# Packs of the last expert stage: the up weights are split in the chunk that a tile needs, and each tile waits for its own chunk

## The reference, cut to what matters

```python
H = D * 2 * 4 // 3          # 682; D = 256
h1 = jnp.einsum('bsd,ehd->ebsh', x, W1)
h2 = jnp.einsum('bsd,ehd->ebsh', x, W2)
eo = jnp.einsum('ebsh,edh->ebsd', jax.nn.sigmoid(h1) * h1 * h2, W3)
out = out + jnp.einsum('ebsd,bse->bsd', eo, weights)
```

## Time and profile before

| | us |
|---|---|
| median of three runs | 2204.55 |
| lowest and highest | 2202.09, 2207.64 |
| profiled execution | 2205.24 |
| its span, first to last instruction | 2203.4 |
| from PE's first up matmul of pack 0 to that of pack 38 | 562.37 |
| one such pack, mean | 14.80 |

### The profile page before, as it was taken

How to read it: one execution, slowest core, us unless ns; L and a number is a source line. 1 busy time by engine, 2 the same in 40 slices (tenths; PEclk the granted TensorE clock), 3 DMA queues, 4 the chain that set the end, 5 groups by cost and what they waited for, 6 DMA issues and landing times. The chain is left out here.

```text
span 2203.4 us, 38903 instructions
## 1 busy us (share of the span) xinstructions
PE 1618.1 (73%) x13182; PEld 1262.8 (57%) x13182; DVE 1422.0 (65%) x2628; ACT 704.8 (32%) x1457; POOL 798.5 (36%) x956
## 2 busy tenths in 40 slices
PE   5956766499975768622948996599588888888881
PEld 3545644377752445411634563488588888888881
DVE  4844555666646655541247885566498888888886
ACT  2311011245531434410312664111244444444440
POOL 1421103620014300103314301188566666666660
PEclk8978788689987887855968997699799999999995
DMA  3464615443116332291225321221355445544525
GB/s 103 161 176 124 184 46 148 157 122 114 48 58 184 73 69 68 61 307 61 63 67 170 104 81 37 68 92 66 140 179 177 155 164 177 173 152 171 181 100 191
DMA packets 286765, 274.02 MB, mean 124 GB/s; under 512 B 59033, under 2 KB 263676, under 8 KB 280958
## 3 DMA queue, kind: packets, MB, share of 16 engines
q1 hardware_dynamic: 274647, 249.09, 36.5%
q0 software_dynamic: 8688, 21.16, 2.7%
q10 hardware_dynamic: 3264, 1.57, 0.4%
HBM read 194.74 MB, written 79.35 MB: 124 GB/s over the span
## 5 line engine op out<-in xcount | busy, mean ns | idle before, releaser
L89 PE MATMUL psum<-e_x_split,e_up_split 128*128 128x256 f32 x2340 | 342.5, 300 | 103.7 <-POOL e_up_split L1788 103.7
L89 PEld LDWEIGHTS psum<-e_x_split,e_up_split 128*128 128x128 f32 x2340 | 319.7, 206 | 110.8 <-issue 87.9
L787 DVE TENSOR_REDUCE a_maxima<-psum 128x2 f32<-128x512 f32 x384 | 257.4, 687 | 160.1 <-PE psum L578 91.9
L1788 POOL TENSOR_TENSOR e_up_split<-e_up_raw,e_up_split 128x512 fp32r<-128x512 f32 x195 | 261.0, 1339 | 214.7 <-ACT e_up_split L1710 213.7
L758 ACT ACTIVATE a_probs<-psum 128x512 f32<-128x512 f32 x384 | 224.8, 598 | 265.6 <-PE psum L600 171.2
L1680 PE MATMUL psum<-e_down_split,e_hidden_split 128*128 128x256 f32 x1170 | 183.5, 295 | 0.8 <-DVE e_down_split L1745 0.8
L1731 ACT ACTIVATE e_silu<-psum 128x256 f32<-128x256 f32 x195 | 75.1, 385 | 325.2 <-PE psum L89 325.2
L1680 PEld LDWEIGHTS psum<-e_down_split,e_hidden_split 128*128 128x128 f32 x1170 | 163.1, 201 | 1.0 <-DVE e_hidden_split L1767 1.0
L578 PE MATMUL psum<-s_k_stack,s_q_stack 96*128 96x256 bf16 x512 | 123.0, 295 | 42.2 <-DMA a_rel_stack<-scr_r 30.0
L1767 DVE TENSOR_TENSOR e_hidden_split<-e_hidden,e_hidden_split 128x256 fp32r<-128x256 f32 x195 | 138.8, 712 | 6.7
L1039 DVE TENSOR_TENSOR a_products<-psum,mask 128x512 f32<-128x512 f32 x128 | 82.9, 686 | 77.6 <-PE psum L972 77.4
(11 more groups left out here) (246 smaller groups left out, 3170.6 us busy)
## 6 DMA issues: line engine op xcount, KB each, us to landing
e_up_raw<-in_w_ffn SPq DMA_DIRECT2D x39, 1280.0 KB, 7.5
e_down_raw<-in_w_ffn SPq DMA_DIRECT2D x39, 640.0 KB, 4.1
scr_q<-p_parts SPq DMA_DIRECT2D x40, 384.0 KB, 2.7
scr_k<-p_parts SPq DMA_DIRECT2D x40, 384.0 KB, 2.8
a_q_stack<-scr_q SPq DMA_DIRECT2D x96, 128.0 KB, 2.9
s_q_stack<-scr_q SPq DMA_DIRECT2D x96, 128.0 KB, 2.7
s_k_stack<-scr_k SPq DMA_DIRECT2D x96, 128.0 KB, 2.7
a_k_stack<-scr_k SPq DMA_DIRECT2D x84, 128.0 KB, 3.0
```

The lines of the kernel that those rows point to most:

```text
L89: last = eng.matmul(out, lhs(a, k), rhs(b, k), start=i == 0, stop=i == len(terms) - 1)
L787: dve.tensor_reduce(MX[:, u // 8, :, u % 8], s_bank(u), AX.X, ALU.max).then_inc(S["s_used"], 1)
L1788: pool.tensor_tensor(SU[:, r, 1, q], RU[:, r, q], SU[:, r, 0, q], ALU.subtract).then_inc(S["up_lo"], 1)
```

## The change

Both `high_up` and `low_up` now treat, as chunk m, the four runs of 128 columns that tile m needs, by a view of the buffer. Each instruction still handles 512 columns of 128 partitions. The view is of both parts of SU (e_up_split) and of RU alike, so that what is read lies where it is written. PE's wait ahead of tile c changes from the low parts of the whole pack to the first c + 1 low parts. No instruction is added, removed or moved on any engine, and all other waits stand, among them those by which ACT waits for a buffer to come free and SP for the low parts of a whole pack.

```diff
+        def tile_of(weights, m):
+            return weights.rearrange("p (w m n) -> p w m n", w=2 * KD, m=n_h)[:, :, m, :]
...
-                    pe.wait_ge(S["up_lo"], (i + 1) * n_h)
+                    pe.wait_ge(S["up_lo"], c + 1)
...
                 def high_up(i, m):
-                    r, q = i % 2, slice(m * UP, (m + 1) * UP)
+                    r = i % 2
...
-                    act.activation(SU[:, r, 0, q], RU[:, r, q], ACT.Copy).then_inc(S["up_hi"], 1)
+                    act.activation(tile_of(SU[:, r, 0], m), tile_of(RU[:, r], m), ACT.Copy).then_inc(S["up_hi"], 1)
...
                 def low_up(i, m):
-                    r, q = i % 2, slice(m * UP, (m + 1) * UP)
+                    r = i % 2
                     pool.wait_ge(S["up_hi"], i * n_h + m + 1)
-                    pool.tensor_tensor(SU[:, r, 1, q], RU[:, r, q], SU[:, r, 0, q], ALU.subtract).then_inc(S["up_lo"], 1)
+                    pool.tensor_tensor(tile_of(SU[:, r, 1], m), tile_of(RU[:, r], m), tile_of(SU[:, r, 0], m), ALU.subtract).then_inc(S["up_lo"], 1)
```

## The result

| | before | after |
|---|---|---|
| median, us | 2205.24 | 2114.30 |
| lowest and highest | 2202.09, 2207.64 | 2106.14, 2116.53 |
| profiled execution | 2205.24 | 2116.53 |
| its span | 2203.4 | 2114.7 |
| PE's first up matmul, pack 0 to pack 38 | 562.37 | 476.68 |

The change makes the kernel faster by 4.2%: the ratio is 0.9582, with a 95% interval of 0.9553 to 0.9610. On a second chip it gave 0.9586 (0.9558 to 0.9613). The forecast was 2133 us, with a range of 2075 to 2182.

A forecast was written before the change was run, and what follows sets the result against it. PE's 2.63 us stall for POOL's last low part was to go, leaving DVE as bound at 13.0 us a pack. Span 2203.4 - 68.4 - 3.0 = 2132.0 us, so a median of 2133 us, range 2075 to 2182.

The forecast's parts named there:

- 13.0 us a pack: Forecast pack time with DVE as bound: 8.84 us of its own work plus 4.2 us held up by POOL.
- The upper bound of 14.1 us: Longest pack if each of five low parts holds DVE in full, 1.06 us each: 8.84 + 5.3 us.
- DVE's idle time of 1.8 us as what can come back: Of PE's 2.63 us stall only DVE's idle 1.8 us a pack returns: 38 x 1.8 = 68.4 us.
- The lower clock has no term of its own: Lower PE clock, up to 1.5 us in two packs of three, gets no term: PE has 1.8 us slack.
- The first pack: At the stage's start PE waits for one low part and the split rows only: 3.0 us come back.
- The four runs: POOL's subtraction over four runs of columns: price between nothing and a factor of 1.41, taken as nothing.
- rival E: Slower: POOL's subtraction pays for the four runs, 1.34 us becomes 1.89, a pack takes 15.75 us; 2238 us, chance 4%.
- A: DVE bound with today's hold-ups, 12.4 to 13.6 us a pack: 2110 to 2156 us, middle 2133; chance 45%.
- B: Hold-ups fall where DVE reads PSUM, interface needs only 11.5 us; 11.6 us a pack, 2080 us, chance 22%.
- C: Each of POOL's low parts holds DVE in full, 14.1 us a pack: 2175 us, chance 20%.
- D: Up weights land late for ACT: at landings of 10.4 us a pack takes 13.7 us, 2160 us; chance 5%.
- F: Change doesn't do what it says: another arrival is as late as the last low part; 2204 us, chance 4%.

The follow-up runs named there:

- pool_quarter: Changed kernel, but from pack 2 on POOL makes the low part of only one of a chunk's four runs; 2057.82 us, ratio 0.9346 to the kernel before.
- after_pe_more: Changed kernel with each pack's four transposes made twice on PE; 2097.51 us, ratio 0.9541 to the kernel before.
- before_fill: Kernel before, with twelve useless PE transposes ahead of the wait at each pack's start; 2160.23 us, ratio 0.9823.
- views_only: Four-run chunks of the change, with PE's old wait for all five low parts; 2198.30 us, ratio 0.9999 to the kernel before.
- wait_only: Kernel before with its old chunks, tile 0 waiting for the first four low parts, other tiles for all five; 2113.62 us, ratio 0.9604.
- after_dve_more: Changed kernel with DVE's copy of a pack's output made twice; 2174.93 us, ratio 0.9897 to the kernel before.
- before_dve_more: Kernel before with DVE's copy of a pack's output made twice; 2236.33 us, ratio 1.0159.

## Why the prediction was right, and where it was off

- **The stall goes, PE is not the next bound, DVE is.** Right, and shown by pool_quarter and after_pe_more, not by the trace alone.
- **13.0 us a pack.** It took 12.54. The own time of 8.84 us was right. The term that was mis-sized is the holds, 4.2 us taken over from the old schedule against 3.7 us measured. I had named this as the thing that could be wrong in size. That it came so near was in part luck: edits that left POOL's and DVE's operations as they were, or added one, moved the holds between 3.3 and 4.7 us, and nothing in my working could tell where in that span they would fall. 0.45 us in 38 packs is the 17 us by which the stage beat the forecast: 562.37 - 476.68 = 85.7 us came back, where I had 68.4.
- **The upper bound of 14.1 us.** It took 1.06 us for a full hold, but the earlier trace rows have a longer one: L1745 takes 1.74 us in place of 0.42, 1.32 over. With that the bound is 8.84 + 5 x 1.32 = 15.4 us. No settled pack of the changed kernel came near it, so the slip did no harm.
- **DVE's idle time of 1.8 us as what can come back.** Half right. It matched the other estimate since both are one account of DVE's time in the same packs, and no check of each other. But the idle time lay in the packs at the lower clock and those with fewer holds. before_fill shows that at full clock DVE was filled for 13.5 of 13.78 us, and that the step from there to the changed kernel came mostly from fewer holds.
- **The lower clock has no term of its own.** Right for the sum, as the mean pack of 14.80 us held its cost, and of no help to a reader who asks where the gain came from: before_fill gives 1.8 of 4.2% to the clock.
- **The first pack.** 3.0 us forecast; the first up matmul starts at 1578.50 against 1581.44, 2.94 us.
- **The four runs.** At nothing, right by views_only. The forecast that POOL's operation keeps its median near 1.29 us was wrong: it is 1386 ns in the changed kernel. As views_only has the same chunks and 1292 ns, it is not the runs. A DVE without pauses isn't enough for it either, as wait_only has that and a median of 1298 ns. What is left is how POOL's operations fall against DVE's, which is argued and not shown. The factor of 1.41 that I kept for rival E was misread: the 335 ns of the earlier trace rows are a mean that five copies of 1.2 to 1.5 us lift, and the median of those copies is 238 ns.
- **What would show it.** DVE's idle time beyond the regular gap: under half a us foretold, 0.2 measured. The sum of the three means: 1.97 us foretold for A and near 1.5 for B, 1.88 measured. PE's waits in the common pack: under 1 us, ahead of the down product, as foretold.
- **The rivals.** B, a mere sharing of the interface at 11.5 us, did not come about: four of five low parts held DVE. As to the rule of the Trainium skill behind it (page "GPSIMD Engine Reference", "Key points"), it names the right operations, and the rows add that a held operation waits for the end of POOL's whole instruction (1.50 us for one of 0.42, beside one of 1.37 on POOL). C, holds in full, came about in after_dve_more in part (4.6 us), so its mechanism was real. D did not: landings took 7.6 us at the median and 8.6 at most, and after the first load ACT waited for none. E and F fell with views_only and wait_only.

## What to carry to other kernels

When a wait is removed, add up the busiest other engine over one period, with its operations at the durations that they have beside their neighbours, and expect the gain to end there. Where two engines exclude each other, price the period as own time plus holds, and treat the holds as a quantity of the schedule: useless transposes on PE moved them by 0.4 us a pack and one more copy by 0.9. Before you call idle time on an engine free, look who waits for what you put there: a copy of 0.7 us on a DVE with 1.8 us idle cost 0.71 us a pack. Then take work off the engine that is held, or shorten the operation that holds it, rather than tune the order.

## What the runs showed of the hardware that was not expected

- Extra work on PE made the kernel faster, 0.9541 against 0.9582 in ratio, and the account puts it down to the phase of POOL against DVE; the two intervals overlap a little, but the packs of the two traces, 12.13 and 12.54 us, and their holds do not.
- A DVE operation can be held by two POOL operations in a row, 3.13 us for one of 0.42, with no turn between them.
- A hold can begin before POOL's subtraction does. In before_dve_more L1769 (0.43 us undisturbed) begins 0.53 us ahead of it, under POOL's write of output rows, and ends behind it; L1745 at 1623.09 in the earlier trace rows is like it. In the changed kernel an operation under the same write was not held, as the second fence shows. What makes the difference stays open.

```profile
1718.77 1.01 POOL L1801 DMA_INDIRECT scr_y<-e_y_pack,e_row_of_slot  x1 [0.64 <-issue]
...
1719.29 2.08 DVE L1769 TENSOR_TENSOR e_hidden_split<-e_hidden,e_hidden_split 128x256 fp32r<-128x256 f32 x1
...
1719.82 1.27 POOL L1790 TENSOR_TENSOR e_up_split<-e_up_raw,e_up_split 128x512 fp32r<-128x512 f32 x1
```
```profile
1916.43 1.01 POOL L1802 DMA_INDIRECT scr_y<-e_y_pack,e_row_of_slot  x1 [0.28 <-issue]
...
1916.63 0.29 DVE L1768 CAST e_hidden_split<-e_hidden 128x256 fp32r<-128x256 f32 x1
```

- Behind the gated product (0.41 us) on DVE, an operation that does not need it starts after 0.33 us, and one that does after 0.52 us.
- A stall of 2.47 us of idle PE a pack came with the lower clock level in two packs of three; with most of the stall filled by useless transposes, and 0.15 + 0.70 us of idle PE left, it came in none.
- Both traces of the changed kernel show two packs of 13.7 to 13.8 us amid those of 12.53. They are packs in which DVE is held for longer; what sets them off stays open.
